# A two-layer graph network kernel: in the first stage the gathered x rows are turned and copied one step ahead

## What is computed

```python
Q = (V[src] @ Wq + bq).reshape(-1, H, HD)          # H = 8 heads of HD = 16
K = (V[dest] @ Wk + bk).reshape(-1, H, HD)
Vv = (V[dest] @ Wv + bv).reshape(-1, H, HD)
bias = E @ Wb + bb
scores = einsum('ehd,ehd->eh', Q, K) / sqrt(HD) + bias
alpha = softmax of scores over the edges of one destination
O = segment_sum(alpha * Vv, dest) @ Wo + bo
x = layernorm(x + O)                                # first layer

h = x @ W
e = leaky_relu(s1[src] + s2[dst], 0.2)              # s1 = h @ a1, s2 = h @ a2
attention = softmax(e)                              # over all edges
x = layernorm(x + segment_sum(attention * h[src], dst))
```

## Time and profile before

| | us |
|---|---|
| median of 3 runs | 1043.37 |
| lowest and highest | 1042.86, 1046.71 |
| span of the profiled execution | 1278.0 |
| busy in it: PE, DVE, ACT, POOL | 729.8, 814.2, 718.6, 760.7 |
| indirect transfers: 196 each of source rows, destination rows, new rows, scatters | 185.1, 186.9, 186.8, 195.8 |

### The profile page before, as it was taken

How to read it: one execution, slowest core, us unless ns; L and a number is a source line. 1 busy time by engine, 2 the same in 40 slices (tenths; PEclk the granted TensorE clock), 3 DMA queues, 4 the chain that set the end, 5 groups by cost and what they waited for, 6 DMA issues and landing times.

```text
span 1278.0 us, 14643 instructions
## 1 busy us (share of the span) xinstructions
PE 729.8 (57%) x3271; PEld 477.8 (37%) x3271; DVE 814.2 (64%) x3724; ACT 718.6 (56%) x2048; POOL 760.7 (60%) x805
## 2 busy tenths in 40 slices
PE   0467777776776776777745455445436534444442
PEld 0335545544544544555544354434422111111110
DVE  5487777776776777777855456555447755565553
ACT  3358777777777777777612333334355544554443
POOL 7565666666666666663166665666625566556665
PEclk9988888778888787778956777776775777667776
DMA  7355575566765666653437667576542222122210
GB/s 211 114 175 169 172 220 166 171 216 186 222 209 179 188 190 184 182 188 115 146 98 219 220 208 226 181 235 199 190 136 75 77 70 72 57 77 67 74 55 28
DMA packets 82017, 196.96 MB, mean 154 GB/s; under 512 B 19802, under 2 KB 21993, under 8 KB 81920
## 3 DMA queue, kind: packets, MB, share of 16 engines
q1 hardware_dynamic: 56746, 148.35, 36.8%
q0 software_dynamic: 25184, 47.69, 13.1%
HBM read 122.78 MB, written 77.22 MB: 156 GB/s over the span
## 4 chain that ended last, share of the span: by engine, by line
DVE 19%; another core or an unknown queue 14%; issue 7%; PE 7%; ACT 5%; DMA 2%; POOL 1%; DVEq 1%; SPq 0%; POOLq 0%
DVE src_b L1449 5%; DVE part L1457 4%; DVE nst L1472 3%; PE psum L727 2%; ACT node_out L780 2%; DMA src_b<-src_t 1%; ACT xsT L941 1%; DVE match L1127 1%; DVE nmv L1482 1%; PE psum L733 1%; POOL out_dram L506 1%; ACT h_res L945 1%; PE psum L755 1%; DMA x1d_in<-x_all 1%
## 5 line engine op out<-in xcount | busy, mean ns | idle before, releaser
L506 POOL DMA_INDIRECT out_dram<-yb,at_last x196 | 195.8, 999 | 144.6 <-ACT yb L780 87.4
L502 POOL DMA_INDIRECT xs<-in_x,src_tab x196 | 185.1, 944 | 154.7 <-remote 71.6
L502 POOL DMA_INDIRECT xs<-x_all,row_tab x196 | 186.8, 953 | 115.1 <-issue 55.5
L502 POOL DMA_INDIRECT h_res<-in_x,dst_tab x196 | 186.9, 954 | 59.7 <-issue 59.7
L755 PE MATMUL psum<-src_b,ident_inv 128*128 128x512 f32 x90 | 74.7, 924 | 146.7 <-DVE src_b L1449 146.7
L780 ACT ACTIVATE h_res<-node_in,shift,rstd 128x128 f32<-128x128 f32 (+1 forms) x392 | 155.7, 482 | 0.3 <-DVE shift L1259 0.3
L941 ACT ACTIVATE xsT<-psum 128x512 f32<-128x512 f32 x48 | 28.6, 597 | 203.0 <-remote 161.9
L585 PE MATMUL psum<-h_res 128*128 128x512 f32 x98 | 72.8, 833 | 119.8 <-ACT h_res L787 119.7
L727 PE MATMUL psum<-w,xsT 128*128 128x129 f32 x384 | 74.8, 356 | 73.5 <-ACT xsT L941 54.7
L780 ACT ACTIVATE yb<-psum,shift,rstd 128x128 f32<-128x128 f32 x198 | 74.5, 456 | 61.5 <-DVE shift L1465 46.1
L589 PE MATMUL psum<-xsT,h_res 128*128 128x512 f32 x98 | 90.1, 1019 | 23.7 <-ACT xsT L791 22.5
(11 more groups left out here) (302 smaller groups left out, 1855.5 us busy)
## 6 DMA issues: line engine op xcount, KB each, us to landing
x1d_in<-x_all SPq DMA_DIRECT2D x98, 256.0 KB
node_in<-in_x SPq DMA_DIRECT2D x48, 512.0 KB
x_all<-h_res SPq DMA_DIRECT2D x48, 512.0 KB
out_dram<-node_out SPq DMA_DIRECT2D x48, 512.0 KB
x_all<-yb SPq DMA_DIRECT2D x49, 256.0 KB
src_b<-src_t SPq DMA_DIRECT2D x49, 256.0 KB
node_in<-x_all SPq DMA_DIRECT2D x24, 512.0 KB
h_res<-in_edge_attr SPq DMA_DIRECT2D x7, 784.0 KB
```

The costliest lines, as they stand in the source:

```text
L502: return pool.indirect_dma_start(out=to, out_offset=None, in_=table, in_offset=bass.IndirectOffsetOnAxis(ap=idx, axis=0))
L506: return pool.indirect_dma_start(out=table, out_offset=bass.IndirectOffsetOnAxis(ap=idx, axis=0), in_=rows, in_offset=None, bounds_check=l ...
```

## The change

In stage one TensorE turns both kinds of rows of group s+1 in step s, right after `queries_of(s)`, and ScalarE copies them in that step too, between `apply_rows(s-3)` and `copy_weighted(s-1)`. `keys(s+1)` and `queries_of(s+1)` follow in the next step. Group 0 is turned and copied ahead of the loop's body. Source rows are now turned and copied ahead of destination rows. The steps 46 to 48 stay.

```diff
--- before.py
+++ after.py
@@ -649,13 +649,16 @@
             mm(bank[7][:, 3 * P:3 * P + D], a_wide[:, 0, :], w1T[:, :], start=True, stop=True)
             mm(bank[7][:, P + D:P + D + 1], w1T[:, :], a_col[:, 0:1], start=True, stop=True).then_inc(prep_pe, 1)
 
+            turn_src(0)
+            turn_dst(0)
             for s in range(TAIL):
-                turn_dst(s)
                 if edge(s - 2):
                     outputs(s - 2)
-                turn_src(s)
                 keys(s)
                 queries_of(s)
+                if s + 1 < TAIL:
+                    turn_src(s + 1)
+                    turn_dst(s + 1)
                 values(s)
                 if s == 1:
                     tr(bank[6][:, 0:P], src_f[:, 0:P], ident[:, :])
@@ -849,14 +852,12 @@
                 if s == 0:
                     act.wait_ge(prep_pe, 1)
                     fn(w1T[:, :], bank[7][:, 0:P], ACT.Copy).then_inc(prep_act, 1)
-                if edge(s):
-                    copy_dst(s)
+                    copy_src(0)
+                    copy_dst(0)
                 if edge(s - 1):
                     weights(s - 1)
                 if s - 3 >= -AHEAD:
                     deviations(s - 3)
-                if edge(s):
-                    copy_src(s)
                 out_half(s - 4 + AHEAD - 1, 1)
                 out_half(s - 4 + AHEAD, 0)
                 if edge(s):
@@ -868,6 +869,9 @@
                     fn(src_turn[:, 0, :], bank[6][:, 0:P], ACT.Copy)
                     fn(src_turn[0:TILES - P, 1, :], bank[6][0:TILES - P, P:2 * P], ACT.Copy).then_inc(prep_act, 1)
                     fn(whole_row[:, :], bank[6][0:H, 2 * P:3 * P], ACT.Copy).then_inc(prep_act, 1)
+                if edge(s) and s + 1 < TAIL:
+                    copy_src(s + 1)
+                    copy_dst(s + 1)
                 if edge(s - 1):
                     copy_weighted(s - 1)
                 if edge(s - 3 + AHEAD) and s < TAIL - 1:
```

## The result

| | before | changed |
|---|---|---|
| median of 20 runs, us | 1045.99 | 1050.62 |
| lowest, us | 1042.86 | 1045.73 |
| profiled execution, span, us | 1278.0 | 1047.6 |

The account below looks back on a forecast made before the run. GpSimd's gathers were taken to end the first stage last, with ScalarE and DVE near their floors. Stage two at 518 instead of 522.2 gave 1043.4 less 0 to 5, so 1040 us, range 1008 to 1051.

Parts of the forecast that it names:

- the two paths of the budget: Stage two's start before the change: counted back from the timed end, 522.2 us; counted forward over 45 gather groups, 519.
- the late signals: Delays before waiting engines go on, in the profiled first stage; taken as absent, or nearly so, in timed runs.
- The step of 9.44 us: First-stage step of before in timed runs: 11.93 less 2.49 us (114.7 over 46 steps), against ScalarE's own 9.10.
- ScalarE's path: First stage paced by ScalarE: 522.2 less 46 x 0.34 puts stage two's start at 506.6 us.
- part 1: In stage one `keys` and `queries_of` no longer wait for this step's copies; ScalarE's step gives back at most 0.34 us.
- The sum: The later of 506.6 and 518 sets stage two's start; 1043.4 less 0 to 5 us gives 1040.
- the gather path: First stage paced by GpSimd's gathers: 519 less 0.9 puts stage two's start at 518 us.
- Part 2: ScalarE's moved copies start `copy_weighted` 1.20 us later, hidden because TensorE reaches that place later (4.2 against 3.5 us).
- Part 3: Turns waiting late for gathers hold `values` and `scores`: one delay of a few microseconds, taken back in last three steps.
- Part 4, the fill: At the start, turning source rows first frees the ring 0.9 us earlier, shortening GpSimd's 5.12 us wait by that.
- Cheaper gathers: Rival, chance 0.38: unrecorded gathers and scatters take 2% to 4% less, so 23 to 35 us are gained.
- TensorE's loop: Rival, chance 0.18: TensorE's changed first-stage chain of 9.84 us becomes the bound, losing 18 us (1061; half so, 1052).

## Why the prediction was wrong

**What bounds the kernel now: half right.** In executions of 1044 to 1048 us GpSimd has no other wait than its 0.30, and most gathers take the 1.2475 that was read (from 496.77 to 498.02 is 1.25), with a mean of 1.26 to 1.27. Stage two starts at 520.31 in before's profile, where the two paths of the budget gave 519 and 522.2. Both came so near by luck, for errors in them cancel. The second started group 4 at 51.01 and gave each group 9.98, where it starts at 44.97 and a group takes 10.1. The first had 21.3 us ahead of the scatters and 1.29 for each, where there are 10.2 and a mean of 1.34 to 1.35 (777.75 to 1041.28). That the late signals are absent where before takes 1043 us is right too. That they are the recording's is wrong: the same kernel takes 1266 to 1277 us unrecorded on some chips. The row of DVE waiting although its own result was ready spoke for late signals; it couldn't say that recording makes them.

**The step of 9.44 us failed.** It was an average, 114.7 us spread over 46 equal steps, and was read as a step in which ScalarE has 0.34 us of slack. There is no such step. There are free ones of 8.85, in which ScalarE is busy 99% (9.10 had been read for its own work), longer ones in which a turn waits for gathered rows, and two early ones in which ScalarE waits for DVE. So nothing was left to gain on ScalarE's path, and part 1 brings nothing. The sum had already said that the gather path ends last (518 against 506.6), so this alone did not turn the sign.

**Part 2, the copies are hidden: right.** Line 619 waits for `copy_weighted` for 0.3 us in all in the changed kernel, from 60 to 480 us.

**Part 3 named the mechanism and priced it at nothing: this is the step that failed.** "Towards the end PE will wait at a turn with `values` and `scores` of the step before queued behind it" is what the trace shows, from 213 us on. But that the last three steps "take it back" was not worked out, and the delay stands in the sum at nothing. What it costs: after a turn that waited, the scores come 3.9 us later and their softmax begins 5.7 us later (452.15 to 457.80), where in before it has begun already. The lag on entering the last steps is 4.0 us in the profile. These steps take 7.9 to 9.6 us each, but before gains from that too, until it meets the last rows. 3.0 us remain (4.3 in the second profile of the changed kernel). With four steps more in before's order the loss is gone.

**Part 4, the fill: wrong.** The 0.9 us rested on GpSimd's wait of 5.12 us at 51.01, which isn't there in an execution of 1044 us: at 49.97 before issues a gather 0.30 us after the last. It belonged to the late signals as much as the waits that were set aside, and should have been set aside with them.

So stage two was forecast at 518 and came at 521.7 and 525.6 in the two profiles. Against before's 520.3 that is 1.4 and 5.3 us later. The lag of 3.0 and 4.3 us is in both. The rest is where the last gather starts (499.60 in before, 498.02 and 500.61 in the changed kernel), which differs from one profile to the next. The forecast's 4 us of gain was the start of one path (522.2) less the changed start of the other (518). By the second path alone before was at 519, so only the 0.9 us of the fill came from the change; with that gone and the lag counted, the sum would have given a loss.

**The rivals.** Cheaper gathers (0.38 of the chances): fallen. The pace is no faster than 1.25 us in executions of 1044 us as well. TensorE's loop: not in the changed kernel, whose line 619 hardly waits and whose `keys` takes 1.02 us in most steps (as at 476.02) and 1.9 in only a few (as at 459.70). The kernel with the turns ahead of `scores` comes near it, with steps over 10 us at the lower clock. The Trainium skill's "TensorE: Matmul & The Clock Gate", "Part 4: PE-mode transpose", says that a transpose doesn't count as busy for the clock in the same way, and by it eight turns in a row would hold the clock down. The changed kernel has eight turns in a row in the same places of every step, and in the free stretch of 104.7 to 148.8 us the granted clock is 1.00: the trace doesn't agree with the rule as it was used there. In the kernel with the turns ahead of `scores` twelve stand in a row, with those of `turn_weighted`, and its clock was the lowest; whether for that reason no run tells. The range's upper end, 1051, was set for this rival; the result lies just below it by another mechanism, which is luck.

**What would show it.** Line 585's waits for the copy are gone, as said. Line 824's are not gone with them: 3.8 us in before and 3.0 in the changed kernel, from 60 to 480 us. That gathers still come 11.9 us apart, with a span near 1278, held on the chip where before takes 1277 us, most steps, and there the change cost 18 us, for which the text had no term: the period isn't GpSimd's alone there, for it waits for the turns that free the ring (line 580, 61.3 us from 60 to 560).

## What to carry to other kernels

Work moved ahead of a wait is only ahead of what it waits for; what is queued behind it is now one whole delivery later. In the middle of a stream that sets the pace this is hidden, and the price is paid once, after the last delivery, as the part of the chain that used to run beside the wait. So count that chain, and the steps that are left to take it back, before calling it nothing; or change the order back a few steps before the end. An average step is no step: before dividing a budget by the count, ask whether steps of two kinds are in it.

## What the runs showed of the hardware

- The same kernel had medians of 1048 and 1049 us on two chips and of 1266 and 1277 us on two others, in timed runs. In the slower ones a matmul group recorded as ended at 311.50 let DVE go on at 316.30, and GpSimd's wait of 2.2 us before each group of gathers ended 0.5 us after that. In the faster ones GpSimd has no such wait. What makes the signals late was not found, nor whether it belongs to the chip: among runs of before of 1043 to 1050 us there was one of 1207.26.
- Where signals are late, small changes of order cost far more: the same change is 1.4% on one chip and 0.35% and 0.15% in the two comparisons at 1046 to 1049 us. And the order of the variants is another one: turns behind values is the mildest at 1277 us (1.003) and the worst at 1048 us (1.0085).
- Where the signals are prompt, 392 gathers of 128 rows go out one behind the other, most 1.25 us apart, with a mean of 1.26 to 1.27, as some take up to 2.5 us. Only with the destination rows ahead GpSimd waits once besides, 1.95 us at 88.30. The last gather starts between 498.02 and 498.86 us in five of nine profiles and between 499.60 and 502.24 in the other four, and these differences are as large as those between the kernels' medians. One profile of a kernel can't place a difference of 2 us; the stretch behind the last gather could.
- The rows of a group land at very different times after its last gather starts: a turn that waited for them started 2.6 us after it at best and 8.8 us after it at 213.53 in the changed kernel.
